# Token sums on VectorE, P5 ahead of P6 in panel 0, one count per late piece of Wo, spread accumulations and paired late statistics in a decoder layer

## What is computed

```python
x = x + attn(_layernorm(x), Wq, Wk, Wv, Wo)      # 32 query heads, 8 key/value heads, rope, causal softmax
x = x + matmul(fake_quant(_layernorm(x)), fake_quant(ctx_4096))
x = x + ffn(_layernorm(x), A_w, B_w, Wq_w, keys) # 64 experts of rank 8, top 16, gated by a softmax
```

## Time and profile before

| | us |
|---|---|
| median of three runs | 1337.3 (1332.65 to 1338.39) |
| profiled execution, its own time | 1336.83 |
| its span | 1335.0 |
| PE busy / DVE / ACT / POOL | 1274.7 / 820.6 / 770.9 / 613.3 |
| mean granted TensorE clock | 0.986 of full |

### The profile page before, as it was taken

One profiled execution on the slowest core, in us unless ns is written; L12 is line 12 of the kernel. 1 busy time (PEld: TensorE's weight loads), 2 busy tenths in 40 slices (PEclk: granted clock), 3 DMA queues, 4 the chain that ended last, 5 costly groups with the idle time before them and its releaser, 6 DMA issues. The chain is left out here.

```text
span 1335.0 us, 19924 instructions
## 1 busy us (share of the span) xinstructions
PE 1274.7 (95%) x7016; PEld 1094.2 (82%) x7025; DVE 820.6 (61%) x1807; ACT 770.9 (58%) x1585; POOL 613.3 (46%) x454
## 2 busy tenths in 40 slices
PE   5899999999999999999999999999799999988998
PEld 4778998888888888888888878888688887665787
DVE  7498224655555556555555565647587688787763
ACT  4322137677767777777777778853233455555540
POOL 4777666678767777677776754310000000111100
PEclk9899999999999999999999999999899999989999
DMA  7033144547759659486485778569673486100001
GB/s 267 9 126 119 64 130 143 178 127 212 206 153 236 194 146 257 124 201 166 119 236 135 172 217 272 188 204 277 214 212 100 141 290 199 46 1 17 33 32 48
DMA packets 117123, 207.42 MB, mean 155 GB/s; under 512 B 10129, under 2 KB 51089, under 8 KB 113441
## 3 DMA queue, kind: packets, MB, share of 16 engines
q1 hardware_dynamic: 112992, 176.79, 40.2%
q0 software_dynamic: 4032, 29.36, 11.8%
HBM read 147.40 MB, written 88.08 MB: 176 GB/s over the span
## 5 line engine op out<-in xcount | busy, mean ns | idle before, releaser
L1234 DVE TENSOR_TENSOR pT_lo<-banks,pT_hi 128x512 fp32r<-128x512 f32 (+1 forms) x192 | 103.6, 595 | 176.5 <-ACT pT_hi L976 176.5
L1628 PE MATMUL banks<-ob_hi,oa_hi 128*128 128x512 f32 x384 | 150.9, 393 | 8.1 <-DVE ob_lo L1271 8.1
L1628 PE MATMUL banks<-ob_lo,oa_hi 128*128 128x512 f32 x384 | 150.4, 392 | 0.0
L1628 PE MATMUL banks<-ob_hi,oa_lo 128*128 128x512 f32 x384 | 150.4, 392 | 0.0
L1586 PE MATMUL banks<-xc,nring_hi_a 128*128 128x512 f32 x448 | 140.0, 394 | 1.3 <-DVE q_made L1184 1.3
L1586 PE MATMUL banks<-xc,nring_hi_b 128*128 128x512 f32 x448 | 139.8, 393 | 0.0
L1825 POOL TENSOR_TENSOR resid<-resid,colterm 128x1024 f32<-128x1024 f32 x8 | 19.7, 2468 | 256.7 <-ACT colterm L1882 172.8
L960 ACT CAST oa_hi<-oraw 128x1024 fp32r<-128x1024 f32 x48 | 50.4, 1050 | 149.3 <-PE banks L1628 134.3
L976 ACT CAST pT_hi<-banks 128x512 fp32r<-128x512 f32 (+1 forms) x192 | 86.5, 526 | 73.9 <-PE banks L1556 73.7
L1243 DVE CUSTOM_DVE_ANT_0 prob<-banks,mask 128x512 f32<-128x512 f32 (+3 forms) x256 | 109.8, 484 | 0.3 <-DVE resid L1162 0.3
L734 POOL TENSOR_TENSOR q_lo<-q_raw,q_hi 128x512 fp32r<-128x512 f32 x64 | 86.4, 1351 | 41.0 <-ACT q_hi L913 41.0
(11 more groups left out here) (245 smaller groups left out, 3466.8 us busy)
## 6 DMA issues: line engine op xcount, KB each, us to landing
q_raw<-qk_dram SPq DMA_DIRECT2D x64, 256.0 KB, 3.9
o_S<-o_st SPq DMA_DIRECT2D x64, 256.0 KB, 4.1
w<-in_L_attn_Wo SPq DMA_DIRECT2D x32, 512.0 KB, 5.4
oraw<-o_S SPq DMA_DIRECT2D x32, 512.0 KB, 3.7
nraw<-in_L_attn_Wq SPq DMA_DIRECT2D x28, 512.0 KB, 5.6
o_S<-o_S POOLq DMA_DIRECT2D x12, 1024.0 KB, 9.8
o_S<-o_N POOLq DMA_DIRECT2D x12, 1024.0 KB, 10.3
resid<-in_x SPq DMA_DIRECT2D x16, 512.0 KB, 6.4
```

Source lines behind the costliest of these rows:

```text
L1234: nc.vector.tensor_tensor(pT[1][:, sl], turned_chunk(turned, mixed, c), as32(pT[0][:, sl]), ALU.subtract).then_inc(pT_lo, 1)
L1628: ins = nc.tensor.matmul(step_bank(m, t), oa[a][:, s % 2, k, t * P:(t + 1) * P], ob[c][:, s % 2, k, :], start=(q == 0 and k == 0 and i == ...
```

## The change

**First panels.** `ORDER` puts (0, P5) ahead of (0, P6). VectorE makes T1 and T2 (`t1`, `t2`), behind T3 and behind eight more `fill_low`; `t2` waits for `w_low(4)`. GpSimd keeps T4 (`t4`), starts `w_low(0)` only when VectorE's three scaled tiles are done (`ln_out_v`), and holds S3 until T1 is complete. Tile 3 is scaled on VectorE (`SCALED`). The first `w_high` stands ahead of ScalarE's tile. Fills 4 and 5 go to banks 6 and 7, and the last four to banks 2 and 3. `keep_p1(1)` and the two halves of (1, P1) are set around the fills 8 to 11. A11 and A10 of panels 2 and 3 are loaded together.

**Output projection.** Each piece of w11 has its own count (the semaphores `w_in` of the panels, at 48), and `step_high` waits for its piece alone. The last four accumulations start at steps 10, 13, 18 and 24 in place of 8, 8, 16, 16.

**Last stage.** Late statistics, roots and scales are made for tiles 4 and 5 together and 6 and 7 together; `copy_turned(4)` stands ahead of the second tile's exponential; GpSimd adds `colterm` to tile t only when `add_product(t - 1)` is done.

```diff
 PANELS, TURNED = 4, 2
 LASTP = PANELS - 1
-ORDER = ([(0, "P1"), (0, "P2"), (1, "P1"), (1, "P2")] + [(s, p) for s in (0, 1) for p in PROD[2:]]
+ORDER = ([(0, "P1"), (0, "P2"), (1, "P1"), (1, "P2"), (0, "P5"), (0, "P6"), (0, "P7"), (0, "P4"), (0, "P3")]
+         + [(1, p) for p in PROD[2:]]
          + [(s, p) for s in range(2, PANELS) for p in PROD])
 AT = {sp: n for n, sp in enumerate(ORDER)}
...
+SCALED = {0: ("v", 1), 1: ("a", 1), 2: ("v", 2), 3: ("v", 3), 4: ("v", 4), 5: ("a", 2), 6: ("v", 5), 7: ("a", 3)}
...
     def fill_bank(f):
-        return banks[:, 2 + f % 4 if f < 24 else 4 + f % 2, :].rearrange("p (k c) -> p k c", c=P)
+        return banks[:, 6 + f % 2 if f in (4, 5) else 2 + f % 4 if f < 24 else 2 + f % 2, :
+                     ].rearrange("p (k c) -> p k c", c=P)
 
...
-                load_wo(w11, 2 * PAIRS, 1, w11_in, q)
+                load_wo(w11, 2 * PAIRS, 1, w_in[q // 4][q % 4], q)
             else:
...
             if s + 2 < PANELS and c == "C10":
-                sp.wait_ge(w_lo, AT[s, "P5"])
-                load_w(s + 2, ("A11",))
-                sp.wait_ge(w_lo, AT[s, "P3"])
-                load_w(s + 2, ("A10",))
+                sp.wait_ge(w_lo, AT[s, "P4"] + 1)
+                load_w(s + 2, ("A11", "A10"))
             if s + 2 < PANELS and c == "C11":
...
 
-        def turn_sum(n):
-            t = n % TPB
-            if n < TPB:
-                pool.wait_ge(t3_sum, TPB)
-                nc.gpsimd.tensor_tensor(right(t, 0), right(t, 0), left(t, 0), ALU.subtract).then_inc(t_sum, 1)
-            elif n < 2 * TPB:
-                pool.wait_ge(t_sum, t + 1)
-                nc.gpsimd.tensor_tensor(left(t, 0), right(t, 1), left(t, 0), ALU.add).then_inc(t_sum, 1)
-            else:
-                pool.wait_ge(t_sum, TPB + t + 1)
-                pool.wait_ge(fill_turned, TPB + t + 1)
-                nc.gpsimd.tensor_tensor(left(t, 1), left(t, 1), left(t, 0), ALU.subtract).then_inc(t_sum, 1)
+        def t4(t):
+            pool.wait_ge(t_sum, 2 * TPB)
+            pool.wait_ge(fill_turned, TPB + t + 1)
+            nc.gpsimd.tensor_tensor(left(t, 1), left(t, 1), left(t, 0), ALU.subtract).then_inc(t_sum, 1)
...
         accumulate_plain(GROUPS - 1)
         accumulate_negated(GROUPS - 1, 0)
-        pool.wait_ge(step_done, PAIRS)
+        pool.wait_ge(step_done, PAIRS + 2)
         accumulate_negated(GROUPS - 2, 1)
+        pool.wait_ge(step_done, PAIRS + 5)
         accumulate_negated(GROUPS - 1, 1)
-        pool.wait_ge(step_done, 2 * PAIRS)
+        pool.wait_ge(step_done, 2 * PAIRS + 2)
         accumulate_negated(GROUPS - 2, 2)
+        pool.wait_ge(step_done, 3 * PAIRS)
         accumulate_negated(GROUPS - 1, 2)
 
...
-                act.wait_ge(w11_in[q // 4], 64)
+                act.wait_ge(w_in[q // 4][q % 4], 16 * (PANELS // 2) + 16)
             elif OUT[m] == "P5":
...
 
+        def t1(t):
+            dve.wait_ge(t3_sum, t + 1)
+            nc.vector.tensor_tensor(right(t, 0), right(t, 0), left(t, 0), ALU.subtract).then_inc(t_sum, 1)
+
+        def t2(t):
+            dve.wait_ge(t_sum, t + 1)
+            dve.wait_ge(w_lo, 5)
+            nc.vector.tensor_tensor(left(t, 0), right(t, 1), left(t, 0), ALU.add).then_inc(t_sum, 1)
+
...
                     if s == 0:
-                        pe.wait_ge(fill_lo, FILLED[p])
+                        pe.wait_ge(fill_lo, FILLED["P6"] if p == "P5" else FILLED[p])
+                if s == 0 and p == "P6":
+                    pe.wait_ge(fill_lo, len(FILLS) - 1 + fb)
                 if p == "P1" and s == LASTP:
...
+            if t >= 1:
+                pool.wait_ge(m_added, 2 * t)
             if t >= 2:
                 pool.wait_ge(v_scaled, t - 1)
...
     def _(act):
-        def late_root(t):
-            act.wait_ge(var2, t - TPB + 1)
-            nc.scalar.activation(lnw[:, 1, t:t + 1], lnw[:, 0, t:t + 1], ACT.Sqrt).then_inc(root2, 1)
+        def late_root(n):
+            act.wait_ge(var2, n + 1)
+            ts = slice(TPB + 2 * n, TPB + 2 * n + 2)
+            nc.scalar.activation(lnw[:, 1, ts], lnw[:, 0, ts], ACT.Sqrt).then_inc(root2, 1)
 
         def scale_tile(t):
 
             act.wait_ge(v_quant, t - 1)
             if t >= TPB:
-                act.wait_ge(scl2, t - TPB + 1)
...
-                late_root(i + 4)
+            if i == 2:
+                late_root(1)
             if i + AHEAD < TT:
                 root(i + AHEAD)
+            if i == 1:
+                copy_turned(i + 3)
             exponentials(i)
             if i + 1 < TT:
                 highs("x", (2 * i + 2, 2 * i + 3))
             if i + 2 < TT:
                 normalise(i + 2)
-            if i + 3 < TT:
+            if 1 < i < TT - 3:
                 copy_turned(i + 3)
...
 
         def late_stats(t):
             row_stats(nc, resid, stats, moments, t, link)
-            row_scale_in(nc, moments, lnw, slice(t, t + 1), var2)
-
-        def late_scale(t):
-            ts = slice(t, t + 1)
-            dve.wait_ge(root2, t - TPB + 1)
+            if t % 2:
+                row_scale_in(nc, moments, lnw, slice(t - 1, t + 1), var2)
+
+        def late_scale(n):
+            ts = slice(TPB + 2 * n, TPB + 2 * n + 2)
+            dve.wait_ge(root2, n + 1)
             row_scale_out(nc, lnw, rstd, ts, link)
             link(nc.vector.tensor_scalar(scl[:, 0, ts], rstd[:, ts], calc[:, 0:1], None, ALU.mult))
             link(nc.vector.tensor_tensor(lnw[:, 2, ts], moments[:, ts, 0], scl[:, 0, ts], ALU.mult))
...
-        late_scale(TPB)
-        late_stats(TPB + 1)
+        late_scale(0)
         for i in range(1, TT):
             if i + AHEAD < TT:
                 row_term(i + AHEAD)
...
             add_out(i - 1)
+            if i == 1:
+                late_stats(TPB + 2)
+                late_stats(TPB + 3)
         low("z", TT - 1)
         add_out(TT - 1)
```

More of the change, by code:

```diff
@@ L807, in _ @@
         w_low(3)
-        for n in range(TPB):
-            turn_sum(n)
+        pool.wait_ge(t_sum, TPB)
         weight_sum(0, "S3")
+        w_low(4)
+        for t in range(TPB):
+            t4(t)
         weight_sum(0, "S2")
-        for n in range(TPB, 2 * TPB):
-            turn_sum(n)
-        w_low(4)
-        for n in range(2 * TPB, 3 * TPB):
-            turn_sum(n)
         for n in range(5, len(ORDER)):
@@ L1010, in _ @@
         root(0)
+        w_high(0)
         ln_scale(1)
-        ln_scale(3)
-        w_high(0)
         for f in range(4):
@@ L1024, in _ @@
         ln_scale(7)
+        w_high(4)
+        keep_p1(1, (0,))
         for f in range(8, 12):
             fill_high(f)
-        keep_p1(1)
-        w_high(4)
-        for f in range(12, 24):
+        keep_p1(1, (1,))
+        for f in range(12, 28):
             fill_high(f)
         w_high(5)
-        for f in range(24, 28):
-            fill_high(f)
         for n in range(6, len(ORDER)):
@@ L1346, in _ @@
         ln_scale(2)
+        ln_scale(3)
         for f in range(8):
@@ L1356, in _ @@
             t3(t)
-        for f in range(8, 24):
+        for t in range(TPB):
+            t1(t)
+        for f in range(8, 16):
+            fill_low(f)
+        for t in range(TPB):
+            t2(t)
+        for f in range(16, 28):
             fill_low(f)
@@ L1360, in _ @@
         c00(0, 0)
+        c00(0, 1)
         keep_u(0, 2, 0)
-        fill_low(24)
-        fill_low(25)
         keep_u(0, 2, 1)
-        fill_low(26)
-        fill_low(27)
-        c00(0, 1)
         keep_u(0, 3, 0)
         keep_u(0, 3, 1)
+        c11(0, 0)
+        c11(0, 1)
         c00(1, 0)
@@ L1635, in _ @@
         product(0, "P2")
+        product(1, "P1", (0,))
         fills(range(8, 12))
-        product(1, "P1")
+        product(1, "P1", (1,))
         fills(range(12, 16))
@@ L1641, in _ @@
         product(1, "P2", (1,))
-        fills(range(20, 24))
-        product(0, "P6", (0,))
-        fills(range(24, 26))
-        product(0, "P6", (1,))
+        fills(range(20, 26))
+        product(0, "P5", (0,))
         fills(range(26, 28))
+        product(0, "P5", (1,))
         for s, p in ORDER[5:-2]:
```

36 lines of the change are left out of this document (17 added, 19 removed).

## The result

The changed kernel takes **1322.3 us** (median of four, 1320.15 to 1322.61) against 1335.7 (four, 1332.65 to 1338.39): a ratio of 0.990, 95% interval 0.987 to 0.992, so 13.4 us less. The profiled execution is the one of 1322.61 us, span 1320.8; that of before had 1335.0. 1320 was forecast.

A forecast was written before the change was run, and what follows sets the result against it. TensorE, busy 95% of the span, was taken as the bound, so only its idle and low-clock time could move: 1336.8 − 10.3 (output projection) − 2.0 (first panels) − 4.2 (last stage) = 1320.3, called 1320; own spread 1314 to 1326.

The forecast's parts named there:

- Output projection, 10.3 us: Step 12: separate counts and spread accumulations remove 7.2 us idle, 0.2 before step 11 and 3.0 of slow clock.
- rivals 2 and 3: Output projection: an accumulation delays a needed load, 10.3 us stays (12 in 100); both do, 1341 (4 in 100).
- the smaller part: Output projection, step 12: the separate counts alone let ScalarE continue at 949.7 instead of 952.6, worth 2.9 us.
- First panels, 2.0 us: First weight panels: net gain of 2 us after clock costs, bounds 6 gained and 3 lost.
- The first product starts near 17.8: Start of the first panels: first product 1.5 to 1.9 us sooner, near 17.8 and not 19.55.
- The wait on `keep_u`: Before (1,P7) in the first panels: a new TensorE wait on VectorE of 6.6 us, ending at 93.5.
- The clock: First panels: slow clock behind waits, charged 1.5 us around 40 us and 1.5 behind the new 6.6 us wait.
- Rival 1: First panels: VectorE's chain costs more than it gives, 3 us lost and not 2 gained, 1325; 11 in 100.
- Last stage, 4.2 us: Last stage: 2.7 gained by the first hidden product, 2.4 given back at gate(0), 3.9 gained at 1227 us.
- gate(0): Last stage, first tile: the second late statistic now stands ahead of this gate; 2.4 us given back there.
- The rival from the rule on shared ports: First panels: GpSimd holds up VectorE's token sums, chain 9 us late, 1329; 2 in 100.
- The row that I put beside the rule: A VectorE instruction on 128x4 elements took 1.59 us while a GpSimd tensor_tensor ran; said to agree with the rule.

The follow-up runs named there:

- warm: The changed kernel with 25 extra identity transposes on TensorE ahead of the first fill: 1321.3 us, ratio 0.988 to the kernel before.
- sums_first: The changed kernel with VectorE's sums and rotations in the first two panels reordered: 1313.2 us against 1337.5 for the kernel before, ratio 0.983.
- after: The kernel with the whole change, against the kernel before: 1322.3 us against 1335.7, ratio 0.990.
- exp_first: The changed kernel with the second tile's exponential ahead of the q1T copy and half an output sum moved into VectorE's wait: 1318.1 us, ratio 0.986 to before.
- no_hold: The changed kernel without GpSimd's last-stage wait for the sums of the tile before: 1326.8 us against 1336.1 for the kernel before, ratio 0.993.
- best: The changed kernel with a further revised VectorE order from sums_first, the transposes of warm and the moves of exp_first: 1308.3 us, ratio 0.979 to before.
- panels: The kernel before with only the first panels' part of the change: 1337.0 us against 1337.5, ratio 1.000.
- last: The kernel before with only the last stage's part of the change: 1332.5 us against 1337.5, ratio 0.997.

## Why the prediction was right, and where it wasn't

- **Output projection, 10.3 us.** 10.6 in the traces, 9.4 with the part alone. What was named as its signs held: no wait, clock at 1.00 (the earlier trace rows had 0.55), accumulations at 937.6 and 954.0 for 937.1 and 953.4. The load issued at 939.6 beside an accumulation took 9.4 us, near the 10.5 at which rivals 2 and 3 decide, and it made ScalarE 0.8 us late with nobody waiting. What the working lacked is the overlap: it gave the counts "the smaller part", 2.9 us, as if the spread carried the rest alone. Alone they gave 3.7 and 1.7.
- **First panels, 2.0 us: the start was mis-sized.** "The first product starts near 17.8": it started at 19.3. The edit did what it says (the eighth fill no longer waits for its bank), but the first fills are paced by TensorE at 0.85 us each after its idling, not by the 0.48 us of later ones. `warm` has the 18.0. Over all traces without the extra transposes the first product starts at 18.8 to 19.9 us with the new start and at 19.1 to 19.8 with the old one, so the edit of the start is worth at most a few tenths.
- **The wait on `keep_u`** was forecast as 6.6 us, ending at 93.5; it is 7.16, ending at 96.8. Of these 3.3 us the start is 1.5, and the last `fill_low` ended at 58.1 and not 56. So the second half of (1, P7) came 1.25 us sooner than in before (VectorE's `keep_u(1, 3, 0)` at 101.33; the earlier trace rows has it at 102.58), where 2 were forecast behind the clock.
- **The clock.** I charged 1.5 us around 40 us; behind the wait of 1.65 us at 39.33 it stayed at 1.00. Behind the new wait, 3.2 us at 0.50 cost 1.6, where I charged 1.5. Two errors of about 1.5 us, start and clock, partly cancelled, and what is left, 0.6 us in the mean of executions, isn't to be told from nothing. Rival 1 did not come: VectorE's chain took back what the part gave, not more.
- **Last stage, 4.2 us: the size is partly luck.** 4.3 in the traces. By its terms: the first hidden product comes 3.3 us earlier within the stage (27.4 to 24.1 us behind its start; 2.7 forecast), the first `expand` only 0.8 (53.6 to 52.8), so 2.5 are given back (2.4 forecast at gate(0)), and from there to the end 3.5 are gained (3.9 forecast). But the clock is in all three, and the sum had no term for it. `sums_first` has the code of after here and a clock of 1.00 throughout; there the stretch that gives back 2.5 gives back 1.0. And at the product behind the output sum the gain of the stage was 2.9 us, not 4.2; the other 1.4 come from there on, where the clock of before is low from 1227.0 to 1230.4 us and that of after isn't. The stage takes 172.6 to 174.3 us in the five traces with the old code, with the clock low for 10 to 16 us, and 166.3 to 170.1 in the five with the new one, with 0 to 11. One wait of 3.12 us on the output sum and none on `q1T` at that tile, as listed. Unseen was that the second tile's exponential now came too late: `exp_first`, with its two moves, takes 3.4 us off.
- **The rival from the rule on shared ports**: no token sum was stretched (four `t1` in 2.49 us, four `t2` in 2.50). GpSimd was held back then, so this isn't evidence against the rule; `no_hold` shows what happens without such a hold. The row that I put beside the rule was misread: the pass of 1.59 us is a TENSOR_SCALAR with one SBUF input, not a pass with two. A row that does bear on two inputs is the 1.37 us of `no_hold` above.
- **The spread of executions** was no term of mine: 2 us in the attention stretch and up to 3.8 in the last stage for the same instructions.

## To carry to other kernels

When two causes end a wait within a few microseconds of each other, cost them as a pair: each alone gives little, and a trace of one only shows which ended last. On an engine that works in order, put a short step that another engine waits for ahead of long steps that nobody waits for yet, and look which long step has idle time to fall in: here a few moved lines on VectorE were worth more than the whole edit of the panels. Price a transpose or matmul at the start of a program by the slow pace, treat a single execution's stage times as good to 2 to 4 us, and look for low stretches of the clock before a difference between two traces is put down to the code.

## What the runs showed of the hardware

**The same wait is followed by a slow clock in one execution and not in another.** The last stage has waits of 1.81, 1.10, 1.08 (1.09) and 0.96 (0.97) us in `after` and in `sums_first`, the latter's kernel being the same there. Windows of after, then of `sums_first` (whose stage begins 6.7 us earlier):

```profile
1160.00:1170.00 10.00, 8.89 (x64) 0.92 0.00 1
1170.00:1180.00 10.00, 10.00 (x72) 0.91 0.01 2
...
1190.00:1200.00 10.00, 7.71 (x39) 0.83 0.01 2
```

```profile
1160.00:1180.00 20.00, 17.43 (x138) 1.00 0.00 1
1180.00:1200.00 20.00, 16.82 (x116) 1.00 0.00 1
```

The stage takes 168.7 and 166.3 us, and 170.1 in `warm`, all for one code; after has the clock low twice in it, `warm` three times before its end, `sums_first` never. Behind 1.87 us at 90 us in `sums_first` the clock fell to 0.50, behind 1.65 us at 39 (after) and 1.70 us at 70 us (`best`) it did not. The waits at 810 us are the closest pairs: it fell behind 1.78 us (after) and 1.69 us (`exp_first`), and not behind 1.73 us (`panels`) and 1.81 us (`last`). The 3.35 and 7.16 us waits each had it fall before they ended. I can't say from these runs what decides for the short ones. The Trainium skill (TensorE: Matmul & The Clock Gate, section What's actually happening) says that the number of slow matmuls at the start varies from run to run of one kernel. That is about the start and not about waits; at the start the traces agree with it, with 17 to 24 transposes at the slow pace in the five traces that have the start of before.

**TensorE starts slow, and the windows table doesn't show it.** In after the transposes stand 0.21 us apart from 13.7 us on and 0.11 apart from 18.2 us on. The table has 1.00 for both paces (here after, 17 to 19 us), and just as well for 0 to 5 us, in which TensorE has no instruction at all:

```profile
17.00:18.00 1.00, 1.00 (x6) 1.00 1.10 349
18.00:19.00 1.00, 1.00 (x11) 1.00 1.11 349
```

The trace has no record of the clock before 18.1 us, so the 1.00 before it is the lack of a record. In all thirteen traces the pace doubles within 0.1 us of the first clock record: at 18.1 us in after, 18.7 in before, 11.6 in `warm` and 12.9 in `best`, where the 25 transposes, with nothing else on TensorE, stand ahead of the fills. So transposes alone were followed by the quick pace here.
